# A one-core Mamba and attention kernel: one written step order per engine replaced by five, with the shared PSUM banks dealt out for each

## The reference, cut to what matters

```
# layer 0: a state-space block, d_inner 512, d_state 16
xr, gate = split(x @ W_in.T);  xr += t_emb
xc = silu(depthwise_conv4(xr) + b_conv)
xn = layernorm(xc) * ln_g + ln_b
Bm, Cm, dt = split(xn @ W_xproj.T);  dt = tanh(dt @ W_dt.T + b_dt) * 0.01
Ad = 1 - dt * tanh(A_log);  Bd = Bm * min(norm(xn), 1)
h = clip(h * Ad + Bd x xn, -10, 10);  y = Cm . h        # scan over 64 tokens
x += ((y + D * xn) * silu(gate)) @ W_out.T
# layer 1: attention, 16 heads of 16, weights demodulated by the style
z = normalise(x * s1);  q, k, v from z
x += (softmax(q k / 4) v) @ w_w.T * w_dc + v @ u_w.T * u_dc
```

## Time and profile before

| | us |
|---|---|
| median of 3 runs (range) | 1849.23 (1847.76 to 1851.75) |
| the profiled execution's own time | 1853.52 |
| its span, first to last instruction | 1851.6 |
| PE busy in the span | 1632.8 (88%) |
| DVE busy | 1335.7 (72%) |
| POOL busy | 1225.8 (66%) |
| ACT busy | 1164.5 (63%) |
| granted TensorE clock, mean of the span | 0.928 |

### The profile page before, as it was taken

The page is one execution under the profiler, slowest core; times in us unless marked ns, Lnnn a source line. Parts: engine busy times, 40 slices in busy tenths (PEclk is TensorE's granted clock), DMA queues, the critical chain, the costliest instruction groups (busy, mean ns, idle before and its releaser), DMA issues. The chain is left out here.

```text
span 1851.6 us, 41471 instructions
## 1 busy us (share of the span) xinstructions
PE 1632.8 (88%) x12460; PEld 1051.0 (57%) x12460; DVE 1335.7 (72%) x2306; ACT 1164.5 (63%) x2921; POOL 1225.8 (66%) x1874
## 2 busy tenths in 40 slices
PE   5346777899999999999999999999999998998775
PEld 5233233466666666666666666666666555555554
DVE  1413587788888888888888888888888888653221
ACT  4555564577777777777777777777777533344332
POOL 1587866787878787888787878787878632222220
PEclk8556877899999999999999999999999999999786
DMA  3014455565566566666555656666665654322100
GB/s 103 21 48 97 99 121 120 139 146 146 149 145 146 146 148 147 150 146 150 144 150 145 152 144 140 151 140 156 140 155 131 156 128 109 95 74 72 52 21 20
DMA packets 222715, 224.27 MB, mean 121 GB/s; under 512 B 54240, under 2 KB 179552, under 8 KB 222496
## 3 DMA queue, kind: packets, MB, share of 16 engines
q1 hardware_dynamic: 222496, 221.62, 49.1%
HBM read 150.36 MB, written 71.17 MB: 120 GB/s over the span
## 5 line engine op out<-in xcount | busy, mean ns | idle before, releaser
L1478 DVE CUSTOM_DVE_ANT_0 gc<-ps_u,gc,hi 128x512 f32<-128x512 f32 x1008 | 777.6, 803 | 70.8 <-PE ps_u L874 51.1
L890 PE MATMUL ps_y<-gc,cms 128*32 128x512 f32 x2048 | 303.3, 627 | 7.3 <-POOL cms L656 7.3
L1160 ACT ACTIVATE a_tap<-a_xr,conv_w 128x128 f32<-128x128 f32 x768 | 245.6, 399 | 12.9 <-DVE a_xr L1410 11.3
L874 PE MATMUL ps_u<-xs_sb,stage 64*128 64x512 bf16 x1024 | 196.9, 433 | 25.0 <-issue 16.4
L534 POOL TENSOR_TENSOR a_tap<-a_tap 128x512 f32<-128x512 f32 x128 | 163.7, 1280 | 37.1 <-ACT a_tap L1160 36.9
L828 PE MATMUL ps<-a_xT,WinT 128*128 128x128 f32 x1024 | 140.2, 295 | 8.4 <-ACT a_z L1177 4.6
L828 PEld LDWEIGHTS ps<-a_xT,WinT 128*128 128x128 f32 x1024 | 132.3, 209 | 21.4 <-issue 17.0
L685 POOL TENSOR_TENSOR c_yg<-c_yd,c_sg 128x512 f32<-128x512 f32 x64 | 81.8, 1277 | 89.6 <-DVE c_sg L1487 83.1
L550 POOL TENSOR_TENSOR a_ve<-a_mv,eps 128x1 f32<-128x1 f32 x64 | 12.3, 192 | 185.9 <-DVE a_mv L1437 185.1
L919 PE MATMUL ps<-WinT,c_xT 128*128 128x512 f32 x256 | 131.6, 638 | 1.8 <-ACT c_xT L1231 1.8
L937 PE MATMUL ps<-WoutT,c_ygT 128*128 128x256 f32 x512 | 129.3, 396 | 1.6 <-ACT c_ygT L1246 1.6
(11 more groups left out here) (168 smaller groups left out, 3683.2 us busy)
## 6 DMA issues: line engine op xcount, KB each, us to landing
xs_sb<-xn_parts SPq DMA_DIRECT2D x256, 192.0 KB
xn_parts<-a_parts SPq DMA_DIRECT2D x128, 192.0 KB, 3.0
skip_d_xn<-a_dx SPq DMA_DIRECT2D x64, 256.0 KB, 2.0
xs_sb<-xn_parts SPq DMA_DIRECT2D x128, 128.0 KB
scan_out<-y_sb SPq DMA_DIRECT2D x256, 64.0 KB
c_dx<-skip_d_xn SPq DMA_DIRECT2D x64, 256.0 KB, 3.2
c_y<-scan_out SPq DMA_DIRECT2D x64, 256.0 KB, 3.2
c_wu<-style_rows SPq DMA_DIRECT2D x128, 128.0 KB, 3.4
```

What stands on the lines that cost most here:

```text
L874: pe.matmul(ps_u[r][t % 2][:, :], weights[:, :, l * STEPS + t], xs_sb[rows, l % 2, t, :], start=True, stop=True).then_inc(s[f"b_u{r}"], 1)
L890: pe.matmul(ps_y[quad:quad + 32, :], cms[:, slice_no(*chain_of(sig, r)) % 2, v, r, 32 * u:32 * (u + 1)], gc[r][:, (2 * u + v) % RING, :], ...
L1160: ins = act.activation(a_tap[:, tap, m, :].rearrange("p (r t) -> p r t", r=2), a_xr[:, m, :, tap:tap + S], ACT.Identity, bias=bias, scale= ...
L1478: dve._custom_dve(bass.dve_ops.TENSOR_ADD_SAT, out=gc[r][:, t % RING, :], in0=ps_u[r][t % 2][:, :], in1=before, s0=hi[:, c % 4, col:col + ...
```

## The change

Each engine's step(i) stays for the steps with all stages; four more lists are written beside it, and phase() picks one by the step's number. In the full list only ACT's c_take_zT moves, from the end of a step to the head of the next. The wait for a shared bank is now kept by take() on PE while the program is built: it waits for all reads registered by the bank's last holder and registers its own; bank numbers differ between the lists. SP's list is not touched. The calls of the lists are cut to what differs most; a_normalise, c_silu and so on are the functions as before.

```diff
+    A_DEPTH = 3
-        def taken(*owners): ...
+        def phase(i, first, second, full, late, last):
+            if i < SCAN_LAG - 1:
+                return first
+            if i < C_LAG:
+                return second
+            if i < TILES + A_DEPTH:
+                return full
+            return late if i <= SCAN_LAG + SCAN_STEPS else last
         # PE
+            held = [[], [], []]
+            def take(b, *reads):
+                for which, count in held[b]:
+                    pe.wait_ge(which, count)
+                held[b] = reads
+                return bank[b]
-            def c_project_qv(n, ps, free):
+            def c_project_qv(n, b):
                 pe.wait_ge(s["c_zT"], at(n))
-                pe.wait_ge(*free)
+                ps = take(b, (s["c_q"], at(n)), (s["c_vs"], at(n)))
+            def first_step(i):
+                a_project_bc(i - 3, 2)
+                a_transpose_xc(i - 2, 1)
+                a_transpose_x(i, 2)
+                a_transpose_bc(i - 3, 2)
+                a_project_in(i, 2)
+            def second_step(i):
+                a_project_bc(i - 3, 0)
+                scan_block(sig, 0)
+                a_transpose_xc(i - 2, 0)
+                a_transpose_x(i, 1)
+                scan_block(sig, 1)
+                scan_block(sig, 2)
+                a_project_in(i, 2)
+                a_transpose_bc(i - 3, 1)
+                scan_block(sig, 3)
             def step(i):
                 scan_block(sig, 0)
-                c_transpose_z(c0 - 2, bank[2], taken(("c_pT1", c0 - 3), ...
+                c_transpose_z(c0 - 2, 2)
...
+            def late_step(i):
+                c_transpose_x(c0, 1)
+                scan_block(sig, 0)
+                c_transpose_z(c0 - 2, 2)
+                c_weigh_v(c0 - 3, 0)
+                c_project_gate(c0, 2)
+                c_transpose_o(c0 - 3, 0)
+                scan_block(sig, 1)
+                c_project_wu(c0 - 3, 0)
+                c_project_qv(c0 - 2, 1)
+                c_project_k(c0 - 2, 2)
+                scan_block(sig, 2)
+                c_scores(c0 - 2, 2, 1)
+                c_transpose_yg(c0, 0)
+                scan_block(sig, 3)
+                c_transpose_v(c0 - 2, 2)
+                c_transpose_p(c0 - 2, 0, 1)
+                c_project_out(c0, 0)
+                c_transpose_p(c0 - 2, 1, 2)
+            def last_step(i):
+                c_transpose_x(c0, 0)
+                c_transpose_z(c0 - 2, 2)
+                c_weigh_v(c0 - 3, 1)
+                c_project_k(c0 - 2, 2)
+                c_project_gate(c0, 0)
+                c_transpose_o(c0 - 3, 1)
+                c_project_qv(c0 - 2, 2)
+                c_project_wu(c0 - 3, 1)
+                c_scores(c0 - 2, 0, 2)
+                c_transpose_yg(c0, 1)
+                c_transpose_v(c0 - 2, 1)
+                c_project_out(c0, 0)
+                c_transpose_p(c0 - 2, 0, 2)
+                c_transpose_p(c0 - 2, 1, 1)
             for i in range(STEP_COUNT):
-                step(i)
+                phase(i, first_step, second_step, step, late_step, last_step)(i)
         # ACT
+            def second_step(i):
+                a_take_tap(i - 1, 3)
+                a_take_xT(i, bank[1])
+                b_take_y(sig - 1)
+                a_take_tap(i - 1, 0)
+                a_take_tap(i - 1, 1)
+                a_second_part(i - 3)
+                a_normalise(i - 2, bank[0])
+                a_take_tap(i, 2)
+                a_take_bcT(i - 3, bank[1])
+                a_tanh(i - 1)
+                a_first_part(i - 2)
+                a_square_sum(i - 2)
             def step(i):
+                c_take_zT(c0 - 2, bank[2])
...
-                c_take_zT(c0 - 1, bank[2])
+            def last_step(i):
...
+                c_exp(c0 - 2, 0)
+                c_block_values(c0 - 2, bank[1])
+                c_exp(c0 - 2, 1)
         # POOL
+            def second_step(i):
+                spread_c(sig)
+                a_scale_b(i - 3)
+                if chain_due(i, 1) is not None:
+                    split_b(chain_due(i, 1))
+                a_half(i - 1, 0)
+                a_half(i - 1, 1)
+                a_var(i - 2)
+                a_second_rest(i - 3)
+                a_root(i - 2)
+                a_bias(i - 2)
+                a_sum(i - 1)
+                a_gain(i - 2)
+                a_shift(i - 2)
+                a_offset(i - 2)
+                a_skip(i - 2)
+                a_norm_root(i - 2)
+                a_first_rest(i - 2)
         # DVE
+            def late_step(i):
...
+                c_silu(c0, bank[2])
...
+                c_scale_v(c0 - 2, bank[1])
+                c_demodulate(c0 - 3, bank[0])
+                c_scale_q(c0 - 2, bank[1])
+                scan_step(sig, 4, 1)
...
```

More of the change, by code:

```diff
@@ L925, in c_transpose_yg @@
                 pe.wait_ge(s["c_yg"], at(n))
-                pe.wait_ge(*free)
+                ps = take(b, (s["c_ygT"], at(n)))
                 for m in range(MC):
@@ L943, in c_transpose_z @@
                 pe.wait_ge(s["c_z"], at(n))
-                pe.wait_ge(*free)
+                ps = take(b, (s["c_zT"], at(n)))
                 for k in range(KC):
@@ L975, in c_transpose_v @@
                 pe.wait_ge(s["c_vd"], at(n))
-                pe.wait_ge(*free)
+                ps = take(b, (s["c_vbd"], at(n)))
                 for r in range(2):
@@ L1002, in c_transpose_p @@
                 pe.wait_ge(s[f"c_e{g}"], at(n))
-                pe.wait_ge(*free)
+                ps = take(b, (s[f"c_pT{g}"], at(n)))
                 for pair in range(HPC // 2):
@@ L1025, in c_transpose_o @@
                 pe.wait_ge(s["c_o"], at(n))
-                pe.wait_ge(*free)
+                ps = take(b, (s["c_oT"], at(n)))
                 for c in range(KC):
@@ L1046, in step @@
                 scan_block(sig, 0)
[L1047 to L1052, removed]
@@ L1053, in step @@
-                a_transpose_x(i, bank[1],
-                              taken(("a_xr", i - 1), ("c_x1", c0 - 1), ("c_ygT", c0 - 1), ("a_z", i - 3),
-                                    ("c_o", c0 - 4)))
-                c_project_k(c0 - 2, bank[2],
-                            taken(("c_zT", c0 - 2), ("c_pT1", c0 - 3), ("c_vbd", c0 - 3), ("c_sub1", c0 - 3),
-                                  ("a_bcT", i - 4), ("c_f", c0 - 4), ("c_oT", c0 - 4)))
-                c_transpose_x(c0, bank[0],
-                              taken(("a_bc", i - 3), ("c_pT0", c0 - 3), ("c_sub0", c0 - 3), ("c_vs", c0 - 3),
-                                    ("c_sg", c0 - 1)))
@@ L1070, in step @@
-                c_transpose_o(c0 - 3, bank[2],
-                              taken(("c_kbd", c0 - 2), ("c_zT", c0 - 2), ("c_pT1", c0 - 3), ("c_vbd", c0 - 3),
-                                    ("c_sub1", c0 - 3), ("a_bcT", i - 4), ("c_f", c0 - 4)))
-                scan_block(sig, 1)
-                c_project_wu(c0 - 3, bank[2],
-                             taken(("c_oT", c0 - 3), ("c_kbd", c0 - 2), ("c_zT", c0 - 2), ("c_pT1", c0 - 3),
-                                   ("c_vbd", c0 - 3), ("c_sub1", c0 - 3), ("a_bcT", i - 4)))
@@ L1086, in step @@
-                c_scores(c0 - 2, bank[0], bank[2],
-                         taken(("c_vs", c0 - 2), ("c_sg", c0), ("c_xT", c0), ("a_bc", i - 3), ("c_pT0", c0 - 3)),
-                         taken(("a_bcT", i - 3), ("c_f", c0 - 3), ("c_oT", c0 - 3), ("c_kbd", c0 - 2),
-                               ("c_zT", c0 - 2), ("c_pT1", c0 - 3), ("c_vbd", c0 - 3)))
-                c_project_out(c0, bank[1],
-                              taken(("c_ygT", c0), ("a_z", i - 2), ("c_o", c0 - 3), ("a_xT", i), ("a_xr", i - 1)))
```

270 lines of the change are left out of this document (205 added, 65 removed).

## The result

The changed kernel takes **1798.58 us** (median of 4 runs, 1796.04 to 1800.45) beside 1850.49 us for the kernel before in the same comparison (1847.76 to 1855.14). The ratio is 0.9717, 95% interval [0.9699, 0.9735]: 2.8% faster. The forecast was 1790, range 1768 to 1813, so it was right in sign, in place and, within its range, in size. The profiled execution took 1796.04 us, span 1794.1, against 1853.52 and 1851.6 before.

What follows compares the result with a forecast made beforehand. 63% of the span was taken as bound by TensorE's own work, with gains possible in the other 687 us. Terms -29 -10 -7 -4 -5 -3 -2 +1 gave -59, so 1790 us from 1849.2, range 1768 to 1813.

Steps and rivals of the forecast that it cites:

- Steps 77 to 80: Last steps: round-trip gaps get work written into them, 14.9 us a step at full clock, 29 us less (bounds 15 to 33).
- the four waits named as gone: Steps 77 to 80: TensorE's waits on c_vbd, c_oT, c_vsT and c_zT were to leave the list.
- Steps 81 and 82: Steps without gate, yg or out to fill in: 17.5 us a step for 22.4, 10 us less for both (bounds 4 and 16).
- Steps 67 to 75: TensorE's waits on v blocks and z mostly filled: 7 us less in 67 to 71, 4 less in 72 to 75.
- Step 76: One step with 6.4 us of gaps for 15.9 of work: 17.5 us expected, 5 less (1 to 6).
- Steps 17 to 66: Full steps: one more satisfied wait, for c_q, in front of busy TensorE, 1 us more (0 to 3).
- Steps 0 to 6: First steps, a chain with four uses of bank 2: 15.4 us a step, 3 us less (6 less to 3 more).
- Steps 7 to 16: DVE unblocked, 11 us less, against two later chain starts at 4.5 each: net 2 less (6 less to 12 more).
- The store_dx path: Steps 7 to 16: load_raw queues behind store_dx, which waits for later a_skip; chain starts at steps 12 and 16 pay 4.5 us each.
- The clock did not stay down: Rival: TensorE's clock stays down in the last steps, 20 us comes back, 1810 us; chance 0.14.
- The scan's start did wait longer: Rival: store_dx path costs all that steps 7 to 16 win, +10 instead of -2, 1802 us; chance 0.12.
- The other two: Rivals: steps 17 to 66 get slower, 1870 us, chance 0.04; nothing happens, waits reappear elsewhere, 1849 us, chance 0.04.

Runs made afterwards that it cites:

- the round trip put back: Changed kernel with projecting out moved ahead of v's transpose in PE's last list; median 1809.37 us, ratio 0.9769.

## Why the prediction was right, point by point

**Steps 77 to 80: right (59.95 for 59.6), by terms that partly cancel.** The clock of 1.00 is as said, and of the four waits named as gone three are (c_vbd, c_oT, c_zT); so is v's transpose behind the copy of the gated y (0.78 for 0.75). The scaling of q and v (0.7) was said to be covered by the w and u projections. It is not: DVE's c_scale_v itself waits for c_fin of the tile before, that is for these projections, so scores still wait 0.7 (c_vsT). In turn the 0.2 and 0.1 kept for the probabilities and the keys did not show, and the work takes 13.3 and not 13.84 us, which no run explains; TensorE is 89% busy and not over 90. Of 28.8 us, 14.4 is TensorE's busy time (67.62 to 53.20), 12.3 of it by the clock (at full clock the old steps would be 4 x 13.84 = 55.4), and 14.4 is idle time. The share of the clock is this execution's: against the old list behind the new late one it was 5.8 of 22.7.

**Steps 81 and 82: -14.0 for -10, by luck.** The gaps are worth less than said: 6.8 us of idle time were kept for both steps and 10.6 stayed, 4.7 of it on the way from the scores to the subtraction, 3.1 on the keys. The clock made up for it: the term kept 0.68, and the steps ran at 0.94 together, so their work took 20.2 us for the 28.2 of the sum. In the other executions with the new last list both steps took 30.7 to 34.7 us, with step 82 at a clock of 0.68 to 0.94.

**Steps 67 to 75: -15.0 for -11.** The waits are as said: 4.9 us were kept for nine steps in the sum, 4.8 came (3.5 in the first five, 1.3 in the last four). What the term missed is that TensorE's busy time falls too, by 3.7 us. **Step 76: -1.9 for -5.** 1.6 us of idle time were kept and 4.2 stayed. It was costed like its neighbours, though it has the late list without the scan that fills it; the last list there gives 18.0.

**Steps 17 to 66: 0 for +1.** The doubled wait for c_q costs nothing that can be seen; the full step is 23.20 as before.

**Steps 0 to 6: wrong in sign.** The walk gave 15.4 us a step; steps 5 and 6 took 15.9 and 16.7. It had the four uses of bank 2 in turn, and they were the bound. What it missed is 0.5 and 1.3 us, 0.9 on the mean. Silu accounts for 0.7 a step, at 1.64 us behind POOL's a_dx for 0.97 before; it is on the way, since DVE takes bc, which frees bank 2, only behind it:

```profile
125.77 1.64 DVE L1578 SCALAR_TENSOR_TENSOR a_xc<-a_th,a_cv 128x512 f32<-128x512 f32 x1 [2.19 <-PE ps L923]
```

A bank that the list leaves idle was not looked for; it is worth 3.4 and 4.2 us in steps 5 and 6, down to the 12.5 that the prediction read as POOL's work.

**Steps 7 to 16: +1.0 for -2, small terms in the wrong place.** The unblocking of DVE was put at -11; from step 8 to 17 all effects together are about -2.3. DVE gains little, since the updates wait for POOL's a_base in place of PE, and silu is twice as long. The store_dx path was put at two chain starts of 4.5 us each. In the trace the first updates of steps 10 and 12 are 34.2 us apart for 36.9 before, those of steps 14 and 16 40.4 for 39.3. store_dx went out 15.9 and 15.1 us behind the first update, not 17, and the raw load was not held by it there, but by the store of b_c_dt. It is at the first chain (step 6 to 8), which was not counted, that store_dx costs some 3 us. The DVE idle of 6.6 us ahead of step 16 came as said, the one ahead of step 12 did not.

**The rivals.** The clock did not stay down: in every run with the last list steps 77 to 80 held 1.00. What the Trainium skill says ("TensorE: Matmul & The Clock Gate", A second HAM failure mode: psum-queue depth-cycling) of banks cycled with small idles did not show in steps 77 to 80, not with the round trip put back either. It may be what step 76 shows, which cycles three banks too, with waits of up to 1.9 us, and ran at 0.85 in four executions; no run tests that. The prediction took the full clock of one execution of 67 to 76 as evidence against the page, and for step 76 that was too little. The scan's start did wait longer, by some 5 us and at its first start alone, of which the store_dx path is some 3. The other two did not happen.

**The number.** The sum was 1.5 us off on the profiles, and that is luck: the terms that promised too much (0 to 6, 7 to 16, 76) miss by 11 us together, those that promised too little by some 10. The worst ends add to -2, not -3, and 1768 is nearly the best end (1766), not half way to it; neither matters here. The rest of the 8.6 us to the median comes from which executions were profiled: that of before lay 4.3 us above the median it was taken from, that of after 2.5 under its own. Two profiles of the changed kernel lie 6.9 us apart, 6.2 of it clock.

## What to carry to other kernels

Write the drain and the fill of a pipeline as lists of their own: where an engine is idle for round trips, something independent written between the two ends is worth the idle time that it fills, and at the end of this kernel it also kept TensorE's clock up: 12.3 of the 28.8 us gained in steps 77 to 80 in one comparison, 5.8 of 22.7 in another. When a list changes, look up for each shared buffer whether another stands idle, and for each queue what the store in front of a critical load waits for. Judge such edits by distances between fixed instructions in the trace, once you know how far they repeat; a median hides 3 us that the clock of one step gives or takes.

## What the runs showed of the hardware

The granted clock dips for single steps in some executions of identical code: step 18 ran at 0.92 or 0.78 (21.15 or 23.3 us), step 76 at 1.00 or 0.85 (20.4 or 22.5), step 82 at 0.94 to 0.68 (15.5 to 19.5). All have gaps in TensorE's work; steps 21 to 66 and 69 to 75 stood at 0.99 or more in all fourteen profiles. Gaps alone do not bring a dip: the new steps 77 to 80, 11% idle, held 1.00 in all twelve profiles that have them. Why a given execution dips is open; nothing here tried it.

DVE's silu with two inputs in SBUF and POOL's full-width products hardly overlap: silu takes 0.63 to 0.69 us where it comes first or alone, 0.97 behind the last 0.4 us of a_parts, 1.5 to 1.65 behind a whole a_dx. The scan update, which reads one input from PSUM, takes 0.77 to 0.81 us in all 1008, with POOL busy 68% of the span.
